# Graph network on one core: eight first-tile one-hots gathered in a row and written between dense units, sums of four groups per PSUM bank, index casts on ScalarE

## The reference

```python
x = _layernorm(x + gat(x))       # attention over edges, 4 heads, softmax by dst
x = _layernorm(x + std_dev(x))   # per dst: sqrt(mean of squared difference)
x = _layernorm(x + gine(x))      # segment_sum(x[src] + edges @ We, dst), then a small MLP
x = _layernorm(x + sage4(x))     # four times: segment_sum(h[src], dst)/deg @ Wl + h @ Wr
```

## Time and profile before

| | us |
|---|---|
| median of 3 runs | 10603.79 (10591.12 to 10607.39) |
| profiled execution, its own time | 10593.45 |
| its span | 10591.6 |

### The profile page before, as it was taken

One profiled execution on the slowest core, in us unless ns is written; L12 is line 12 of the kernel. 1 busy time (PEld: TensorE's weight loads), 2 busy tenths in 40 slices (PEclk: granted clock), 3 DMA queues, 4 the chain that ended last, 5 costly groups with the idle time before them and its releaser, 6 DMA issues.

```text
span 10591.6 us, 264936 instructions
## 1 busy us (share of the span) xinstructions
PE 7210.5 (68%) x70314; PEld 5219.5 (49%) x70315; DVE 4954.3 (47%) x13673; ACT 1823.6 (17%) x3608; POOL 4603.7 (43%) x4467
## 2 busy tenths in 40 slices
PE   5888788777736666667778766666776555555676
PEld 4666566555512221114445455555665444444666
DVE  4555555444478777774443333333233332322433
ACT  2333333333202335540000000000000000000000
POOL 3777666554400000007540064436444664543754
PEclk7899888888868889997889877776777776667777
DMA  3444333333301122335555655555556666556666
GB/s 67 97 95 89 89 85 83 82 80 74 69 29 49 73 97 121 133 158 157 164 166 178 205 192 180 187 203 172 200 199 217 222 237 220 176 200 223 202 227 219
DMA packets 973363, 1566.12 MB, mean 148 GB/s; under 512 B 499841, under 2 KB 621441, under 8 KB 966402
## 3 DMA queue, kind: packets, MB, share of 16 engines
q1 hardware_dynamic: 485762, 1244.14, 33.2%
q0 software_dynamic: 150016, 196.43, 9.1%
q10 hardware_dynamic: 337280, 122.87, 4.5%
HBM read 1337.91 MB, written 225.00 MB: 148 GB/s over the span
## 4 chain that ended last, share of the span: by engine, by line
PE 41%; issue 18%; DVE 17%; DVEq 13%; DMA 6%; POOL 3%; ACT 2%; SPq 0%; ACTq 0%; POOLq 0%
PE ps_turn L970 19%; PE ps_out L818 6%; PE ps_turn L926 4%; DMA ARENA<-counts 4%; POOL ARENA L657 3%; DVE onehots L1780 3%; DVEq L1794 2%; PE ps_pair L818 2%; PE ps_turn L791 2%; DVE ARENA L1698 2%; DVE ARENA L1700 2%; DMA ARENA<-edge_attr 2%; PE ps_pair L998 1%; PE ps_turn L729 1%; PE ps_out L733 1%
## 5 line engine op out<-in xcount | busy, mean ns | idle before, releaser
L970 PE MATMUL ps_turn<-ARENA 128*128 128x192 bf16 (+2 forms) x28812 | 2708.3, 260 | 550.6 <-issue 200.3
L970 PEld LDWEIGHTS ps_turn<-ARENA 128*128 128x128 bf16 x28812 | 2266.9, 104 | 986.7 <-issue 675.6
L657 POOL DMA_INDIRECT ARENA<-table_sage,idx x1920 | 1901.2, 990 | 1615.6 <-DVE idx L1775 1076.7
L657 POOL DMA_INDIRECT ARENA<-table_gat,idx x1568 | 1732.0, 1105 | 1048.3 <-DMA idx<-src_r 559.8
L998 PE MATMUL ps_pair<-ARENA,onehots 128*128 128x64 bf16 (+2 forms) x12168 | 820.7, 225 | 1097.3 <-DVE ARENA L1787 962.1
L926 PE MATMUL ps_turn<-ARENA 128*128 128x392 bf16 (+1 forms) x4204 | 1064.5, 360 | 677.3 <-DVE ARENA L1700 353.4
L998 PEld LDWEIGHTS ps_pair<-ARENA,onehots 128*128 x12168 | 671.1, 116 | 1253.3 <-issue 1250.5
L657 POOL DMA_INDIRECT ARENA<-table_dev,idx x480 | 475.0, 990 | 1757.6 <-DVE idx L1775 1620.7
L1698 DVE TENSOR_SCALAR ARENA<-ARENA 128x784 bf16<-128x784 f16 (+1 forms) x2102 | 1007.3, 479 | 362.4 <-issue 233.0
L1826 DVE TENSOR_REDUCE DSUM<-ps_turn 128x64 f32<-128x192 f32 (+2 forms) x686 | 264.7, 386 | 1947.8 <-PE ps_turn L970 1838.7
L1780 DVE SCALAR_TENSOR_TENSOR onehots<-DST,TBASE,COL 128x512 f32 x1014 | 763.5, 753 | 652.7 <-issue 651.3
(11 more groups left out here) (296 smaller groups left out, 5865.9 us busy)
## 6 DMA issues: line engine op xcount, KB each, us to landing
ARENA<-counts SPq DMA_DIRECT2D x1764, 448.0 KB
counts<-ARENA SPq DMA_DIRECT2D x49, 3136.0 KB, 9.0
ARENA<-counts SPq DMA_DIRECT2D x588, 224.0 KB
ARENA<-dst_b SPq DMA_DIRECT2D x393, 256.0 KB
ARENA<-edge_attr ACTq DMA_DIRECT2D x392, 128.0 KB
ARENA<-table_sage,idx POOLq DMA_INDIRECT x1920
ARENA<-table_gat,idx POOLq DMA_INDIRECT x1568
nodes_dev<-table_rows ACTq DMA_DIRECT2D x14, 672.0 KB
```

Of the source, the lines that this page charges most:

```text
L657: pool.indirect_dma_start(ps["buf"][:, s, c, 0:ps["row"]], None, ps["table"][:, :], bass.IndirectOffsetOnAxis(idx[:, s, c:c + 1], 0)).then ...
L970: last = pe.matmul(ps_dense[half][:, 0:n], RING[:, b, :], XP[:, b, :], start=(b == PIECE_AT[pieces[0]]), stop=(j == pieces[-1] and b == PI ...
```

## The change

TensorE's part of a round is rewritten. It goes in two halves of four groups. In a half the first tiles of the four groups come first, each 12 matmuls from its own place in `tile_hots` (eight one-hots in a row) into its own 128 columns of a bank of `ps_pair`, so that four groups share one bank; there is one wait for the one-hots and one for each group's gathered rows, and none for adds. Then come the further tiles of these groups (`lo + 1` to `hi`), with a ring of two one-hots (`more_hots`) and two banks (`ps_more`, which is `ps_out`). A tiny matmul at the end of the half says that its slots are read (`slots_read`).

VectorE writes the eight one-hots of the coming round in two portions of four (`hots_behind`), each ahead of `take_dense` of half 0 in the units since the last round; what is missing is written at the round. In the round it does the further tiles as before, one pair late, and at the end of each half the four adds of the first tiles.

ScalarE takes over the casts of the indices: one copy for the four groups of a half, when `slots_read` says so, and two at the start of a pass. GpSimd waits once for four slots.

For the space, `onehots` of the first pass moves into that pass's area, the arena grows by 1024 columns, the area of slots shrinks by 1024, and `DST` and `SPAN` get eight groups more, as one-hots are also written for a round behind the last. The diff, cut to `pass_dense` and what it calls:

```diff
-        XP_AT, RING_AT, SLOTS_AT, INDEX_AT = 4 * UNIT, 4 * UNIT + 9408, 4 * UNIT + 9408 + 6272, 4 * UNIT + 9408 + 6272 + 4096
...
         onehot_rest_h = onehot_rest_flat.bitcast(BF16)[:, 0:C * P].rearrange("p (c v) -> p c v", c=C)
-        onehot_ring = onehots[:, :, :].rearrange("p q v -> p (q v)").bitcast(BF16)
+        tile_hots = arena(SLOTS * GE // 2, dt=BF16, at=HOTS_AT)
...
+        ps_more = ps_out
...
                 with pool.Fori(0, pool.value_load(INFO[0:1, 1:2], min_val=1, max_val=ROUNDS)) as i:
                     for s in range(SLOTS):
-                        pool.reg_add(taken_slots, taken_slots, 1)
-                        pool.wait_ge(ps["slots_free"], pool.snap(taken_slots, min_val=1, max_val=8 * GROUPS))
-                        settle(pool)
+                        if s % 4 == 0:
+                            pool.reg_add(taken_slots, taken_slots, 1)
+                            pool.wait_ge(ps["slots_free"], pool.snap(taken_slots, min_val=1, max_val=8 * GROUPS))
+                            settle(pool)
                         gather(ps, s)
-                pool.reg_add(taken_slots, taken_slots, SLOTS - 1)
+                pool.reg_add(taken_slots, taken_slots, 2)
...
-                    for s in range(SLOTS):
-                        lo, hi = load_four(pe, spans, s, r * SLOTS + s)
-                        pe.wait_ge(ps["gathered"][s], pe.snap(arrived, min_val=1, max_val=len(passes) * ROUNDS * 16 * C))
+                    for h in range(2):
+                        pe.reg_add(made, made, SLOTS // 2)
+                        pe.wait_ge(tile_hot, pe.snap(made, min_val=1, max_val=8 * GROUPS))
                         settle(pe)
-                        with pe.Fori(lo, hi) as t:
-                            pe.reg_add(seen, seen, 1)
-                            count = pe.snap(seen, min_val=1, max_val=len(passes) * GROUPS * TILES)
-                            pe.wait_ge(pair_hot, count)
+                        for q in range(4):
+                            pe.wait_ge(ps["gathered"][4 * h + q], pe.snap(arrived, min_val=1, max_val=len(passes) * ROUNDS * 16 * C))
                             settle(pe)
-                            pe.wait_ge(pair_acc, count)
-                            settle(pe)
-                            hot = onehot_ring[:, bass.ds(pe.snap(turn, min_val=0, max_val=1024), GE)]
-                            sums = ps_pair[:, bass.ds(pe.snap(bank, min_val=0, max_val=512), n)]
                             for c in range(C):
-                                for q in range(3):
-                                    last = pe.matmul(sums, hot[:, c * P:(c + 1) * P], buf[:, s, c, q * n:(q + 1) * n],
-                                                     start=(c == 0 and q == 0), stop=(c == C - 1 and q == 2))
-                            last.then_inc(pair_agg, 1)
-                            pe.reg_alu(turn, turn, 1024, ALU.bitwise_xor)
-                            pe.reg_alu(bank, bank, 512, ALU.bitwise_xor)
+                                for part in range(3):
+                                    last = pe.matmul(ps_pair[:, (4 * h + q) * P:(4 * h + q) * P + n], tile_hots[:, ((4 * h + q) * C + c) * P:((4 * h + q) * C + c + 1) * P],
+                                                     buf[:, 4 * h + q, c, part * n:(part + 1) * n],
+                                                     start=(c == 0 and part == 0), stop=(c == C - 1 and part == 2))
+                            last.then_inc(tile_agg, 1)
+                        for q in range(4):
+                            lo, hi = load_four(pe, spans, q, r * SLOTS + (4 * h + q))
+                            with pe.If(lo + 1 < hi):
+                                with pe.Fori(lo + 1, hi) as t:
+                                    pe.reg_add(seen, seen, 1)
+                                    pe.wait_ge(more_hot, pe.snap(seen, min_val=1, max_val=len(passes) * GROUPS * TILES))
+                                    settle(pe)
+                                    hot = more_hots[:, bass.ds(pe.snap(turn, min_val=0, max_val=GE), GE)]
+                                    sums = ps_more[:, bass.ds(pe.snap(turn, min_val=0, max_val=GE), n)]
+                                    for c in range(C):
+                                        for part in range(3):
+                                            last = pe.matmul(sums, hot[:, c * P:(c + 1) * P], buf[:, 4 * h + q, c, part * n:(part + 1) * n],
+                                                             start=(c == 0 and part == 0), stop=(c == C - 1 and part == 2))
+                                    last.then_inc(more_agg, 1)
+                                    pe.reg_alu(turn, turn, GE, ALU.bitwise_xor)
+                        pe.matmul(ps_turn[:, 0:4], ZERO[:, :], ZERO[:, 0:4], start=True, stop=True).then_inc(slots_read, 1)
+                    pe.reg_mov(beyond, 0)
...
+                def count_hots():
+
+                    pe.reg_add(beyond, beyond, SLOTS // 2)
+                    pe.reg_alu(beyond, beyond, SLOTS, ALU.min)
...
                                 if half == 0:
+                                    count_hots()
                                     cold_rounds(pe, turns, r0, cold_round)
+                    pe.reg_add(made, made, beyond)
...
+            def take_indices(k, h, r):
+
+                act.activation(idx[:, 4 * h:4 * h + 4, :].rearrange("p s c -> p (s c)"), SRC16[:, bass.ds(r * ROUND_COLS + h * 4 * C, 4 * C)],
+                               ACT.Copy).then_inc(passes[k]["slots_free"], 1)
...
+                begin_turns(act, turns)
+                for h in range(2):
+                    take_indices(k, h, r0)
+                return r0
...
+                def one(r):
+
+                    for h in range(2):
+                        act.reg_add(slots_seen, slots_seen, 1)
+                        act.wait_ge(slots_read, act.snap(slots_seen, min_val=1, max_val=8 * GROUPS))
+                        settle(act)
+                        take_indices(k, h, r + 1)
+
+                cold_rounds(act, turns, r0, one)
...
+                        begin_step(act, turns, b)
+                        with act.Fori(0, TB):
+                            further_indices(k, r0)
...
-                def take_indices(s, g):
-
-                    ve.tensor_copy(idx[:, s, :], SRC16[:, bass.ds(g * C, C)]).then_inc(ps["slots_free"], 1)
-
...
-                    ring = onehot_ring[:, bass.ds(ve.snap(turn, min_val=0, max_val=1024), GE)].rearrange("p (c v) -> p c v", c=C)
-                    return ve.scalar_tensor_tensor(ring, DST[:, bass.ds(cols, C)].unsqueeze(2).broadcast_to([P, C, P]),
+                def hot(ring, cols, t):
...
+                def add(t, sums):
+
+                    ve.reg_add(adds, adds, 1)
+                    ve.wait_ge(pair_acc, ve.snap(adds, min_val=1, max_val=len(passes) * GROUPS * TILES))
+                    settle(ve)
+                    a = acc[:, bass.ds(t, 1), :]
+                    ve.tensor_tensor(a, a, sums.unsqueeze(1), ALU.add).then_inc(pair_acc, 1)
+
+                def add_waiting():
+
+                    ve.reg_alu(bank, turn, GE, ALU.bitwise_xor)
+                    add(ve.snap(prev, min_val=0, max_val=TILES), ps_more[:, bass.ds(ve.snap(bank, min_val=0, max_val=GE), n)])
+
+                def make_hots(h):
+
+                    g = ve.snap(coming, min_val=0, max_val=ROUNDS) * SLOTS + h * (SLOTS // 2)
+                    for q in range(4):
+                        lo, _ = load_four(ve, spans, q, nc.s_assert_within(g + q, 0, GROUPS + SLOTS - 1, skip_runtime_bounds_check_because="coming <= ROUNDS, h < 2"))
+                        hot(tile_hots[:, bass.ds(h * (4 * GE) + q * GE, GE)], (g + q) * C + C, lo).then_inc(tile_hot, 1)
+
+                def hots_behind():
+
+                    with ve.If(ve.snap(made, min_val=0, max_val=2) < 2):
+                        make_hots(ve.snap(made, min_val=0, max_val=1))
+                        ve.reg_add(made, made, 1)
 
                 def cold_round(r):
 
-                    for s in range(SLOTS):
...
-                            ve.reg_add(pairs, pairs, 1)
-                            count = ve.snap(pairs, min_val=1, max_val=len(passes) * GROUPS * TILES)
-                            hot(g * C + C, t).then_inc(pair_hot, 1)
-                            ve.wait_ge(pair_agg, count)
-                            settle(ve)
-                            ve.wait_ge(pair_acc, count)
-                            settle(ve)
-                            add().then_inc(pair_acc, 1)
-                            ve.reg_mov(prev, t)
-                            ve.reg_alu(turn, turn, 1024, ALU.bitwise_xor)
-                            ve.reg_alu(bank, bank, 512, ALU.bitwise_xor)
-                        take_indices((s - 1) % SLOTS, g + (SLOTS - 1))
+                    with ve.If(ve.snap(made, min_val=0, max_val=2) < 2):
+                        with ve.Fori(ve.snap(made, min_val=0, max_val=2), 2) as h:
```

(23 more changed lines are left out.)

91 lines of the change are left out of this document (54 added, 37 removed).

## The result

The changed kernel takes **10340.3 us** (median; 10337.0 to 10348.2), the kernel before 10600.9 in the same comparison: **ratio 0.9757, 95% interval 0.9745 to 0.9769**, 260 us faster. The forecast was 10460. The profiled execution has a span of 10336.9 us against 10591.6.

The account below looks back on a forecast made before the run. No engine was taken as simply full, with GpSimd's gathers a second bound close by. 317 + 3 - 63 - 113 = 144 us off 10593.5 gave 10449; the median lies 10 above: 10460, range 10310 to 10690.

Parts of the forecast that it names:

- Part 1: TensorE's rounds of steps 3 to 7: a round takes 15.5 us at 64 columns; 317 us saved in all.
- Part 2: Rounds of steps 1 and 2, at GpSimd's pace: almost no change, taken as 3 us gained (bounds -40, +40).
- Parts 3 and 4: VectorE: tile adds after the last tile cost 63 us at step ends; one-hots ahead of take_dense cost 113 us.
- further tiles with branches and loads: In a TensorE round: 5.3 us for 3.3 further tiles, 1.9 for eight branches, 1.0 for two span loads.
- the branches: Eight new ones in a TensorE round: about 0.4 us for each of 4.7 skipped, 0.25 else, put at 1.9 us.
- First tiles, first wait and exit: In a TensorE round: 5.1 us for 96 matmuls at 1.2 GHz, 1.0 for first wait and late VectorE, 1.2 exit.
- the wait for gathers: Rounds after three units in sage2 and sage3: GpSimd's second half comes 3.3 us late, eight times, 26 us lost.
- third rival: The clock stays up: 2.4 us less in the first unit after each of 54 rounds, 130 us, 10330; chance 0.13.
- the sign named ahead of the run: L722's wait after a round would be 1.5 us longer if the forecast was right.
- One-hots late enough to stop mid-step units: Four one-hots before the half 0 read cost 8 us, not 4.4, and units wait for PSUM: 10800; chance 0.12.
- A handshake as pace: Rounds on TensorE take 19 us and not 15.5, 189 us less saved: 10640; chance 0.16.
- GpSimd as the bound of all rounds: Landing and restart in halves stretch GpSimd's 40.6 us to 46: 10750 at worst, half of it 10670; chance 0.09.

Follow-up runs that it names:

- no_further: Changed kernel with the further tiles of the groups left out of the computation on both engines: 10073.5 us, ratio 0.9496.
- half_gather: Changed kernel with GpSimd issuing two of the four gathers of a group, the matmuls reading them twice: 9961.4 us, ratio 0.9392.
- late: Changed kernel with one line moved, so VectorE writes the four one-hots behind the read of a unit's first half: 10250.8 us, ratio 0.9674.
- no_ahead: Changed kernel with no one-hots written between dense units; VectorE writes all eight at the start of the round: 10432.3 us, ratio 0.9842.
- one_by_one: Changed kernel with the shared bank undone: first tiles alternate between two banks, TensorE waiting for the sum two tiles back: 10644.2 us, ratio 1.0032.
- load8: Against the kernel with late one-hots and release by two groups (10177.1 us): TensorE loads all eight groups' spans at the round's head; 10205.0 us.

## Why the prediction was right, and where its terms were off

The sign and the mechanism held; the size was 116 us short: 144 forecast, 260 measured (255 in the spans, 251 in the six passes). By the table 73 of it is in the later rounds (390 for the 317 of Part 1) and 36 in the rounds of steps 1 and 2 (39 for the 3 of Part 2). The dense runs at starts took what Parts 3 and 4 had in sum (177 for 176), but not for the reasons given there.

**Part 1, the round at 15.5 us: the mis-sized term.** Mid-step rounds are 12.7. no_further splits them: the further tiles with branches and loads are 8.6, where I had 5.3 + 1.9 + 1.0 = 8.2 (for 3.3 of them, and these rounds have 3). By my own prices the branches come to 2.7 and not 1.9 (4.7 x 0.4 + 3.3 x 0.25), so a correct sum would have read 16.3 and been further off. First tiles, first wait and exit are 4.1, where I had 5.1 + 1.0 + 1.2 = 7.3. Part of that error is the clock, since I took the lower level for all first tiles, and the first wait is gone as well at 64 columns. Windows of two whole mid-step rounds, one of sage1 and one of sage4 (length, then busy PE, PEld, DVE, ACT and POOL, granted clock, DMA), and below them the second first-tile stream of that round of sage4, L999 alone:

```profile
7367.50:7377.90 10.40, 4.84 (x125) 4.23 (x124) 3.58 (x12) 0.43 (x2) 3.73 (x4) 0.98 0.47 174
9858.40:9869.30 10.90, 5.85 (x123) 5.16 (x118) 3.86 (x13) 0.43 (x2) 4.06 (x5) 0.84 0.52 189
...
9863.00:9865.80 2.80, 2.72 (x48) 2.59 (x48) 0.50 0.15 41
```

The round of the kernel before that the one of sage1 answers to, L998 alone:

```profile
7456.30:7475.10 18.80, 8.00 (x120) 6.48 (x120) 0.54 0.33 101
```

The round begins at the upper level that the dense run left. In sage1's round it lasts nearly to the end (0.98, against 0.54 before); in sage4's the second stream is already at the lower one. At 2.4 GHz 48 matmuls take 1.56 us, at 1.2 GHz 2.72. Sage1's round is one of only three with a clock above 0.95: the 24 mid-step rounds have 0.78 on average (0.60 to 1.00), those of the kernel before 0.61. The first stream is at the upper level in all twelve with 64 columns, the second takes 2.72 us in eight of them and 2.43 on average.

Both streams together are therefore 4.0 us there, against the 5.1 of the sum: 1.1 of the 2.8 us by which 15.5 was too long is the clock, 1.0 the first wait, and the rest is not divided by any run. With two further tiles in each, sage4's round is only 0.7 us longer than sage1's (10.9 and 10.2 from dense end to dense start).

So 9.2 us are saved in mid-step and not 5 to 7.4. Over all 54 later rounds it is 390 us, against 317: the missing 73. The rounds at the ends of steps save only 5.6 (25.7 to 20.0, without the last of all). Of the 3.5 us between the two, the wait for gathers is 2.0: with half the gathers these rounds are at 18.0. The longer wait for node work (2.2 to 2.6 us in 15 of the 30) would be some 1.2 on average, an estimate from those rows. I had put the wait for gathers at 26 us for sage2 and sage3 alone, and half_gather shows it in all six passes.

**The clock.** The third rival named a cause that is there, at the wrong place and at too high a price. It had 2.4 us in the first unit behind a round. That unit did not change: behind the round of sage1 93 matmuls take 9.00 us at 0.83 of the clock in the changed kernel and 89 take 8.90 at 0.81 before, and all other dense runs and node work sum to the same (2174.7 and 2174.3). What the clock gives is inside the round. That the time came out near this rival's 10330 is a coincidence.

```profile
7378.00:7387.00 9.00, 9.00 (x93) 8.76 (x93) 3.93 (x8) 0.00 (x0) 6.93 (x7) 0.83 0.64 179
```

```profile
7475.10:7484.00 8.90, 8.90 (x89) 8.71 (x90) 0.64 (x2) 0.00 (x0) 6.77 (x8) 0.81 0.62 179
```

The Trainium skill ("TensorE: Matmul & The Clock Gate", section "What's actually happening") has activity as what releases the throttle; these rows agree (0.54 in the sparse round before, 0.81 in the dense unit behind it). They show beside it that the upper level outlasts the first part of a sparse stretch, the first stream of every mid-step round with 64 columns, and now and then all of it.

**Part 2, steps 1 and 2.** Forecast 3 us gained. From the start of a pass to the start of step 3 the six passes differ by 0.3 us in sum (for gine, whose first dense run can't be told from dev's last, from its first round on): dev -8, gine -3, the others +1 to +4. The rounds there fall by 39 us and the dense runs grow by as much; half_gather shows that GpSimd holds both. Its mechanism stands. But the sum as a whole then counted these steps twice: Parts 3 and 4 charge the tail and the one-hots to the start of step 2 too, 6 x 1.5 + 3 x 4.4 + 5.6 = 28 us by my prices, although Part 2 has GpSimd set the end of these steps. Measured, 45 of the 177 us at starts belong to the first runs of passes and of step 2, and the 39 us in the rounds pay for them.

**Parts 3 and 4, tail and one-hots.** Forecast 63 + 113 = 176 us, measured at starts 177, but shared otherwise: late takes away 82 of the one-hots' part and no_ahead 97 (I had 113), and 79 remain for the tail and the starts of passes (I had 63). In sage4's rows the tail is 2.5 us (I had 1.5) and the one-hots 4.2 (I had 4.4). The tail is the second mis-sized term, since the starts do not even hold all of it: in gine, sage1 and sage3 the node work's wait behind a round grew by 2.2 to 2.6 us, where the sign named ahead of the run was 1.5. That the sums agree is luck. At step starts alone sage4 grows by 48 us, dev by 42, sage2 by 34 and gine by 30, while sage1 and sage3 do not change (-1 and 0): I had seen part of the price in all six.

**The other rivals.** One-hots late enough to stop mid-step units: other dense runs did not grow, so no. A handshake as pace, 19 us: mid-step rounds are 12.7. GpSimd as the bound of all rounds: half true; without it (half_gather) the later rounds are 59 us shorter, so it takes 2 us from each of the 30 at ends of steps, not all of the gain.

**Open.** The first dense runs of sage1 and sage4 are 7.5 us longer in the changed kernel (35.0 and 36.3 us; 27.2 and 28.8 before), and nearly as much in late (35.9 and 34.6). Most of it is one pause behind their first unit, in which TensorE waited for nothing that the profile shows. no_further does not have it (27.6 and 27.3 us). The start of sage1 in the changed kernel, then in no_further:

```profile
7034.78 18.80 PE L977 MATMUL ps_turn<-ARENA 128*128 128x192 bf16 x196 [6.04 <-issue]
```

```profile
6939.07 8.26 PE L977 MATMUL ps_turn<-ARENA 128*128 128x192 bf16 x98 [0.19 <-issue]
```

So leaving out the code of the further tiles removes the pause; why is open. How one_by_one's loss divides between bank and order was not tried apart.

## What to carry over

When work is written ahead for a later stage, put it behind the read that another engine is waiting for: the same one-hots cost 82 us more in front of it than behind it, and behind it perhaps still 15. When a sparse stretch between dense ones is shortened, price the part that follows the dense run at once at the upper clock and the rest mostly at the lower, and read the granted clock of many such stretches, as a single one (0.98 here, with a mean of 0.78) can mislead. Price each cost only where the engine that bears it sets the time. And where a queue of gathers is the bound, its first release and the work left behind its last landing set the time, so the grain of release is to be tried on both sides (halves, pairs, single groups: 10251, 10177, 10205).

## What the hardware showed that I had not expected

- One-hots of 128x512 write back to back at 0.66 us apart (four in 2.74 us, a single one 0.75), but 2 to 3 us of issue stand ahead of each four in the changed kernel, where the program has loads of spans, registers and a semaphore. In the rows above that is 2.96 at the step start.
- A register load that seems to stand on TensorE's path may cost little where it is and 0.9 us at the head of the round (load8: 0.90 of issue before the first stream with 64 columns; mid-step rounds 13.8 against 13.4 us in all). It is not seen in dev, where the first stream of these rounds starts with no gap.
- GpSimd's gathers keep their pace once they run: 975 ns each in the changed kernel, and in sage1 93 in a row start between 7061.9 and 7179.8, one every 1.28 us, as before the change (96 in 122.6 us). ScalarE's cast for four groups takes 0.22 us.
